# Attention scores computed twice in 32x64 tiles over four row strips and four PSUM banks, with norm rows on GpSimd

## The reference

```python
h = (tok_table[x] + pos_table + seg_table[seg]) * 16          # seg: cummax(x == 102)
h = h + attn(layernorm(h))
h = h + ffn(layernorm(h))
# attn: Q, K, V = x@wq, x@wk, x@wv in 16 heads of 16; a query sees the 64 keys up to itself
#   p = softmax(Q K^T / 4 masked to the window); local = p V
#   8 latent heads of 16 over 64 latents (means of 8 tokens of x@wgk, x@wgv), masked to the past
#   rem = softmax(GQ GK^T / 4) GV @ r_out_w
#   out = (sigmoid(Q.gate_l) * local + sigmoid(Q.gate_r) * rem) @ w_out
# ffn: each of 8 experts takes, in turn, the 2048 free tokens with the highest score norm(x)@centroid,
#   then routed + gelu(layernorm(routed)@w1 + b1)@w2 + b2, put back in the order of the tokens
```

## Time and profile before

| | |
|---|---|
| median of 3 runs | 5002.72 us (4962.28 to 5036.0) |
| span of the profiled execution | 4945.8 us |
| PE busy | 4629.6 us (94%), 27948 matmul records |
| PEld busy | 3051.0 us (62%) |
| DVE busy | 2406.4 us (49%) |
| ACT busy | 1623.1 us (33%) |
| POOL busy | 739.8 us (15%) |

### The profile page before, as it was taken

The page is one execution under the profiler, slowest core; times in us unless marked ns, Lnnn a source line. Parts: engine busy times, 40 slices in busy tenths (PEclk is TensorE's granted clock), DMA queues, the critical chain, the costliest instruction groups (busy, mean ns, idle before and its releaser), DMA issues. The chain is left out here.

```text
span 4945.8 us, 80440 instructions
## 1 busy us (share of the span) xinstructions
PE 4629.6 (94%) x27948; PEld 3051.0 (62%) x27948; DVE 2406.4 (49%) x7255; ACT 1623.1 (33%) x3333; POOL 739.8 (15%) x817
## 2 busy tenths in 40 slices
PE   5999999999999999999999999999996699999999
PEld 3666666666666666666666666666664366665666
DVE  4444444444444444534444444444445766666661
ACT  2333333333333333323333333333332233333333
POOL 1000000000000000100000000000000244444443
PEclk8777676776767676868676776767676799999999
DMA  1000000000000000000000000000000011111111
GB/s 36 14 10 10 10 11 10 10 9 10 11 10 9 10 11 10 15 9 11 10 11 10 10 10 10 10 10 10 10 11 27 20 51 52 47 50 51 48 42 41
DMA packets 52864, 94.25 MB, mean 19 GB/s; under 512 B 9116, under 2 KB 37736, under 8 KB 52488
## 3 DMA queue, kind: packets, MB, share of 16 engines
q0 software_dynamic: 18816, 51.41, 3.7%
q1 hardware_dynamic: 33672, 37.87, 2.3%
HBM read 55.68 MB, written 33.55 MB: 18 GB/s over the span
## 5 line engine op out<-in xcount | busy, mean ns | idle before, releaser
L1320 DVE TENSOR_REDUCE mx<-S_ps 128x4 f32<-128x512 f32 (+1 forms) x640 | 442.7, 692 | 1343.1 <-PE S_ps L914 1102.9
L914 PE MATMUL S_ps<-Kt,Qt 32*64 32x128 f32 (+1 forms) x6144 | 1090.7, 374 | 0.0
L687 ACT ACTIVATE probT<-T_ps 128x512 f32<-128x512 f32 x640 | 382.2, 597 | 1919.9 <-PE T_ps L963 1916.6
L914 PEld LDWEIGHTS S_ps<-Kt,Qt 32*64 32x64 f32 (+1 forms) x6144 | 634.0, 186 | 532.9 <-issue 463.9
L963 PE MATMUL T_ps<-cst,prob 128*128 128x128 f32 x2560 | 564.6, 360 | 0.0
L963 PEld LDWEIGHTS T_ps<-cst,prob 128*128 128x128 f32 x2560 | 381.9, 181 | 230.2 <-issue 230.2
L847 PE MATMUL S_ps<-hT,w 128*128 128x512 f32 x1024 | 474.7, 610 | 17.1 <-ACT hT L654 12.1
L860 PE MATMUL O_ps<-w,hid 128*128 128x256 f32 x2048 | 460.3, 379 | 0.0
L1321 DVE TENSOR_TENSOR prob<-S_ps,mx 128x512 f32<-128x512 f32 x640 | 442.6, 692 | 21.8
L936 PEld LDWEIGHTS O_ps<-Ve,probT 128*64 128x64 f32 x4096 | 359.8, 172 | 124.9 <-issue 124.9
L691 ACT ACTIVATE prob<-prob 128x512 f32<-128x512 f32 x640 | 401.0, 627 | 102.6 <-DVE prob L1321 102.2
(11 more groups left out here) (205 smaller groups left out, 5913.3 us busy)
## 6 DMA issues: line engine op xcount, KB each, us to landing
h_rows<-h SPq DMA_DIRECT2D x128, 128.0 KB, 1.7
w<-in_w SPq DMA_DIRECT2D x16, 1024.0 KB, 6.1
rows<-in_tok_table,idx_now POOLq DMA_INDIRECT x136, 3.6
out_rows<-orow,idx_cur POOLq DMA_INDIRECT x128, 2.4
b<-in_b SPq DMA_DIRECT2D x8, 128.0 KB, 5.1
hrow<-h_rows,idx_next POOLq DMA_INDIRECT x64, 2.8
hrow<-h_rows,idx_cur POOLq DMA_INDIRECT x64, 2.7
P<-in_pos_table SPq DMA_DIRECT2D x1, 512.0 KB
```

What stands on the lines that cost most here:

```text
L687: nc.scalar.activation(probT[u % 2][:, :], T_ps[u % 2][:, :], ACT.Copy).then_inc(s_pT, 1)
L914: mm = nc.tensor.matmul(cols[lo:hi, n:n + 2, a, :], Qt[par][r:r + 32, c, t * P + lo:t * P + hi], Kt[par][r:r + 32, c, block, :, :], start= ...
L1320: chain(dve, nc.vector.tensor_reduce(top, sc, AX.X, ALU.max), base)
```

## The change

The scores are computed twice, and the transposes of the probabilities go away. A sequence now has five units instead of 20: unit 0 is the latent heads of all four tiles, units 1 to 4 are all 16 heads of one tile each. A unit fills four PSUM banks (`banks`, formerly `S_ps` and `T_ps`), bank `g` from the 32 rows of strip `g` of the array.

First, `top_scores` computes the scores with queries on the partitions; DVE takes only their maxima (`dve_tops`, two instructions over 1024 columns each). PE transposes the maxima (task MX, eight output rows), ACT negates them into `low` or `lowl`, and SP copies them by DMA into a spare row of the queries. The matching row of the keys holds ones, so that a product of keys and queries has the maximum already taken off. Then `key_scores` computes the scores again, with keys on the partitions, into the same four banks, and ACT takes the exponential of them straight into `probT` (`act_exp`, two instructions over 1024 columns each). L1321, L963, L687 and the separate `scores` are gone. Masks are laid by bf16 matmuls of 32 rows and 64 output columns, 16 for each pass.

For each sequence, PE's program for the scores was 16 x (1 + 6) + 4 x 2 = 120 matmuls and 80 transposes. In the changed kernel `top_scores` is 16 masks and 64 matmuls of 64 columns for the latents, and 16 masks and 32 matmuls of 128 columns for each tile; `key_scores` is 16 masks and 8 matmuls of 512 columns for the latents, and 16 masks, 16 matmuls of 128 columns and 32 of 64 columns for each tile. That makes 160 masks, 392 fp32 matmuls and no transpose. All have the tile shape 32 x 64.

The other edits: `plan` has ten entries, two for each unit (one between `top_scores` and `key_scores`, one behind). The values of a whole tile are one task (VAL: 32 matmuls for heads and 8 for latents). POOL applies the norms itself (`pool_norm`, `pool_y`) and embeds two sequences ahead (`AHEAD`, `HB`, four buffers `hres`). Q, G and PK are written by ACT twice, once for each parity of the head. The loop's body is four sequences.

```diff
-RING = 4
-T_LAG = 2
-O_LAG = 3
+AHEAD = 3
+HB = 4
...
+        TAKER = {"ET": "A", "RT": "A", "RO": "D", "MT": "A", "WO": "D", "YT": "A", "SC": "D", "MX": "A",
+                 "Q": "A", "K": "A", "G": "A", "PK": "A", "PV": "D", "V": "A"}
...
+        plan = [
+            [("MT", 1), ("ET", 0), ("ET", 1), ("VAL", 2), ("ET", 2), ("ET", 3), ("YT", 0), ("WO", 1), ("MX", 0)],
+            [("RT", 2), ("Q", 0), ("SC", 0), ("RO", 2)],
+            [("MT", 2), ("VAL", 3), ("YT", 1), ("WO", 2), ("MX", 1)],
+            [("RT", 3), ("Q", 1), ("SC", 1), ("RO", 3)],
+            [("MT", 3), ("G", 0), ("PK", 0), ("YT", 2), ("WO", 3), ("MX", 2)],
+            [("K", 0), ("V", 0), ("SC", 2)],
+            [("VAL", 0), ("YT", 3), ("MX", 3)],
+            [("RT", 0), ("K", 1), ("PV", 0), ("SC", 3), ("RO", 0)],
+            [("MT", 0), ("VAL", 1), ("WO", 0), ("MX", 4)],
+            [("RT", 1), ("V", 1), ("V", 2), ("V", 3), ("RO", 1)],
+        ]
...
+                        if name == "MX" and m.here(task):
...
+                            sp.wait_ge(s_mA, m.out(task))
...
+                                    sp.dma_start(Qt[q % 2][HD * (1 - j)::32, j, :, (s - 1) * P:s * P],
+                                                 low[(s - 1) % 2][j::2, :, :]).then_inc(s_low[s], 16)
...
+        def pool_norm(pool, n, t, hb, m):
...
+            nc.gpsimd.tensor_tensor(out=rs0[:, t:t + 1], in0=ve0[:, t:t + 1], in1=mhalf[:, :],
+                                    op=ALU.pow).then_inc(s_rs0, 1)
...
+            nc.gpsimd.tensor_scalar(xn[:, t, :], hres[:, hb, t, :], mv0[:, t, 0:1], rs0[:, t:t + 1],
+                                    ALU.subtract, ALU.mult).then_inc(s_xn, 1)
...
+                            pool_y(pool, TS * (b - lag(task)), t)
...
+                    nc.scalar.activation(low[(t - 1) % 2][:, :, :], bank[0:2 * G, 0:KC * P].rearrange("p (c k) -> p c k", c=KC),
+                                         ACT.Copy, scale=-1.0).then_inc(s_mA, 1)
...
-                nc.scalar.activation(Qt[nx][:, t, :], bank[:, :], ACT.Copy, scale=HD ** -0.5).then_inc(s_mA, 1)
...
+                for j in range(2):
+                    ins_ = nc.scalar.activation(Qt[nx][:, j, t, :], bank[:, :], ACT.Copy, scale=c_query[:, j:j + 1])
+                ins_.then_inc(s_mA, 1)
...
+                    ins_ = nc.scalar.activation(Kt[nx][:, j, t, W:], bank[:, :], ACT.Identity,
+                                                scale=c_parity[:, j:j + 1], bias=c_unit[:, j:j + 1])
...
+        def act_exp(act, k, u, pair):
+
+            act.wait_ge(s_ST, 2 * k + pair + 1)
+            dst = latT if u == 0 else probT[(u - 1) % 2]
+            nc.scalar.activation(dst[:, 2 * pair:2 * pair + 2, :], banks[:, 2 * pair:2 * pair + 2, :],
+                                 ACT.Exp).then_inc(s_exp, 1)
...
-                        act.wait_ge(s_T, NUB * (b - back) + u + 1)
-                        nc.scalar.activation(probT[u % 2][:, :], T_ps[u % 2][:, :], ACT.Copy).then_inc(s_pT, 1)
...
-                        act.wait_ge(s_shift, 2 + NUB * b + s + 1)
-                        nc.scalar.activation(prob[:, s % RING, :], prob[:, s % RING, :], ACT.Exp).then_inc(s_exp, 1)
...
+                    first, rest = plan[2 * s + 1][0], plan[2 * s + 1][1:]
+                    run = m.old if s == 0 else m.new
+                    if run:
+                        act_exp(act, NU * b + s - 1, (s - 1) % NU, 0)
+                    act_misc(act, m, first, b, nx)
+                    if run:
+                        act_exp(act, NU * b + s - 1, (s - 1) % NU, 1)
+                    for task in rest:
+                        act_misc(act, m, task, b, nx)
...
+            elif name == "MX":
...
+                pe.wait_ge(s_max, 2 * (NU * b + t + 1))
+                if t == 0:
+                    tops = mxl[:, :].rearrange("p (g j t) -> p t (g j)", g=G, t=TS)
+                else:
+                    tops = mx[:, t % 2, :].rearrange("p (g j c) -> p c (g j)", g=G, c=KC)
+                for n in range(TS if t == 0 else KC):
+                    mm = nc.tensor.transpose(bank[0:2 * G, n * P:(n + 1) * P], tops[:, n, :], c_ident)
...
+            def top_scores(m, b, par, s):
...
+                if not (isinstance(b, int) and NU * b + s < 2):
+                    pe.wait_ge(s_exp, 2 * (NU * b + s - 1))
+                t = s - 1
+                for r in range(2):
+                    for g in range(G):
+                        for a in range(2):
...
+                                nc.tensor.matmul(banks[side[a], g, :].rearrange("p (h k) -> p h k", h=G),
+                                                 onehot[strip[g], r, :],
+                                                 by_query[strip[g], min(t, 1) if a == 0 else 1, r, :].unsqueeze(1)
+                                                 .to_broadcast([32, G, P]), start=r == 0, stop=False)
+                for n in range(2 * TS if s == 0 else G):
+                    j, c = divmod(n, TS if s == 0 else KC)
+                    for g in range(G):
+                        for a in range(2):
...
+                                at_ = t * P + a * W
+                                mm = nc.tensor.matmul(banks[side[a], g, n * P:(n + 1) * P],
+                                                      Qt[par][strip[g], j, c, at_:at_ + W],
+                                                      Kt[par][strip[g], j, c, at_:at_ + P],
+                                                      start=False, stop=n == G - 1)
+                        if g % 2 and n == (2 * TS if s == 0 else G) - 1:
+                            mm.then_inc(s_S, 1)
...
+            def key_scores(b, par, u, drained):
...
+                pe.wait_ge(s_max, drained)
+                pe.wait_ge(s_low[u], 32 * b + 32)
+                t = u - 1
...
+                if u == 0:
+                    for j in range(2):
+                        for g in range(G):
+                            mm = nc.tensor.matmul(banks[side[j], g, :], Gk[par][strip[g], j, :], Gq[par][strip[g], j, :],
+                                                  start=False, stop=True)
+                            if j and g % 2:
+                                mm.then_inc(s_ST, 1)
...
+                        nc.tensor.matmul(banks[side[0], g, n * P:(n + 1) * P], k[:, W + at_:P + at_], q[:, at_:at_ + P],
+                                         start=False, stop=n == G - 1)
+                        nc.tensor.matmul(banks[side[1], g, n * P:n * P + W], k[:, at_:W + at_], q[:, at_:at_ + W],
+                                         start=False, stop=False)
...
+                        mm = nc.tensor.matmul(banks[side[1], g, n * P + W:(n + 1) * P], k[:, P + at_:P + W + at_],
+                                              q[:, at_ + W:at_ + P], start=False, stop=n == G - 1)
+                        if n == G - 1 and g % 2:
+                            mm.then_inc(s_ST, 1)
...
+                        top_scores(m, b, par, s)
+                    half(2 * s)
+                    if m.old if s == 0 else m.new:
+                        drained = 2 * (NU * b + s + 1) if m.new else 2 * NU * SEQS
+                        if s == 0:
+                            key_scores(b - 1, 1 - par, NU - 1, drained)
+                        else:
+                            key_scores(b, par, s - 1, drained)
+                    half(2 * s + 1)
...
+        def dve_tops(dve, k, s):
+
+            for pair in range(2):
+                dve.wait_ge(s_S, 2 * k + pair + 1)
+                width = H if s == 0 else 2 * G
+                tops = mxl[:, pair * H:(pair + 1) * H] if s == 0 else mx[:, s % 2, pair * 2 * G:(pair + 1) * 2 * G]
+                nc.vector.tensor_reduce(tops.rearrange("p (g h) -> p g h", g=2),
+                                        banks[:, 2 * pair:2 * pair + 2, :].rearrange("p g (h k) -> p g h k", h=width // 2),
+                                        AX.X, ALU.max).then_inc(s_max, 1)
```

More of the change, by code:

```diff
@@ new lines, in _, with sequence @@
+            for t in range(TS):
+                pool_gather_rows(pool, 2, t)
+            for t in range(TS):
+                pool_norm(pool, 1, t, 1, Misc("head"))
+            def sequence(b, q):
+                m = Misc(b, q % 2)
+                ahead = not isinstance(b, int) or b + 2 < SEQS
+                for n, half in enumerate(plan):
+                    if ahead and n in EMBED_AT:
+                        pool_gather_rows(pool, b + 3, EMBED_AT[n])
+                    if ahead and n in NORM_AT:
+                        pool_norm(pool, b + 2, NORM_AT[n], (q + 2) % HB, m)
+                    for task in half:
@@ L711, in pe_misc @@
             name, t = task
-            if not m.here(task):
+            if name == "VAL" or not m.here(task):
                 return
@@ L926, in values @@
[L926 to L944 removed]
+            strip = [slice(32 * g, 32 * (g + 1)) for g in range(G)]
```

592 lines of the change are left out of this document (292 added, 300 removed).

## The result

| | before | after |
|---|---|---|
| median | 5009.3 us (4962.28 to 5036.0, 4 runs) | 3423.22 us (3416.55 to 3430.15, 4 runs) |
| span of the profiled execution | 4945.8 us | 3414.8 us |

A forecast was written before the change was run, and what follows sets the result against it. PE bounds the attention loop, 83.5 us a sequence at full clock. Kept work 37.7, scores 16, transposes 1.8 and waits 9.6 make 65 us, 78.3 at clock 0.78; 32 x 78.3 + 1234.4 + 57 gives 3800 us, range 3560 to 4350.

The forecast's parts named there:

- the clock: PE in the attention loop: mean clock 0.78, the trace's best sequences, so a sequence takes 78.3 us.
- the prediction's own formula: Attention sequence time 1/(w/65 + (1-w)/106), with w the time share at full clock and mean clock 0.5 + 0.5w.
- the share of projections grows: Reason given for attention's 0.78 clock: projections ran at 1.00 and fill more of a sequence as scores shrink.
- the 57 us: Whole kernel: median 5002.7 us over profiled span 4945.8 us, added to the new span of 3740 us.
- full clock throughout: Rival on PE's attention clock: full clock all the time, 3370 us; given no chance of its own.
- Under 3560, by a clock over 0.89: Outcome for the whole kernel: under 3560 us because PE's clock exceeds 0.89; chance 0.08.
- The scores: PE's score blocks: 12.8 us over eight tiles, raised to 13.8 by issue, plus 2.2 for shape changes: 16 us a sequence.
- within 1.5 to 2 us: Sign in PE's timeline: a tile's score block takes this long at full clock, matmul starts some 25 ns apart.
- The waits: PE waiting in attention for ACT's read-outs of Q, K, V and the bank for G and PK: 9.6 us a sequence.
- Work and waits at full clock: PE in an attention sequence: 55.5 us of work plus 9.6 us of waits, 65 us at full clock.
- POOL's norm rows and the small DMA releasing nobody: Sign in the attention profile: POOL's norms, 12 us more a sequence, and the maxima's DMA stay hidden.
- each late row would show on PE as a wait on `xn` or `y`: Attention norms moved to POOL: without several us of cover per row, PE would wait on these buffers.

The follow-up runs named there:

- strips in turn: Changed kernel with each block's score matmuls issued one row strip after another, masks and products the same: 5418.27 us, 1.10 of before.

## Why the prediction failed, and where it held

**The step that failed is the clock.** It says "so I take the better value, 0.78: w = 0.56 and 78.3 us". Measured: 0.957, so w = 0.91. Put into the prediction's own formula this gives 1 / (0.91/65 + 0.09/106) = 67.4 us, and 68.0 us were measured. The reason given, that the share of projections grows, is a small part: a tenth more work of that kind gave a clock of 0.74, and the time lost to the clock stayed as it was. What it left out is that the new scores, though each of their matmuls is narrow, would not hold the clock down when all four strips work at once: the same products keep the clock at 0.96 with four strips at once and at 0.64 with the strips in turn. How much of before's low clock was due to its scores and how much to its transposes stays open. The clock makes (78.3 - 68.0) x 32 = 330 us of the 377 us between forecast and measurement; most of the rest is the 57 us below. The rival "full clock throughout" (3370 us) was the nearest and had no chance of its own; "Under 3560, by a clock over 0.89" got 0.08.

**The scores** were sized at 16 us and take 17.3 us; a tile's block "within 1.5 to 2 us" takes 1.55 and 1.86 us. The pace of 25 ns of the earlier trace rows held in the latent `top_scores` (80 matmuls in 1.94 us, 24 ns each). It is 32 ns in a tile's `top_scores` (48 in 1.55 us) and 29 ns in its `key_scores`; the latent `key_scores`, with products over 512 columns, takes 1.77 us for 24. The Trainium skill ("TensorE: Matmul & The Clock Gate", "Wait — 56ns, not 53.3ns?") has 62 ns a matmul with hardware decode off; by that, an estimate, the 64 matmuls of a block would take 4 us. The trace has 1.86 us, so that pace doesn't bind in this run.

**The waits** were named rightly, with the read-outs of Q, K, G and V, but each is shorter than counted (1.0 against 1.6 us in RO), and K's stands in SC (L825) and not in RO. PE's in the sequence at 277.10:

```profile
PE M_ps L809 <- ACT Qt L673: 2.0, 2, 1.0
PE M_ps L825 <- ACT Kt L678: 1.7, 2, 1.1
PE M_ps L821 <- ACT Gq L683: 1.0, 1, 1.0
PE M_ps L806 <- DVE h L1208: 0.9, 2, 0.6
PE M_ps L844 <- ACT gt L695: 0.8, 1, 0.8
```

With the small ones some 7 us, for which 9.6 us were counted. Work and waits at full clock were forecast at 65 us, and the sequence takes 63.6 us. So that step held, in its mechanism and, within 2.5 us a term, in its sizes.

**Hidden by other work.** "POOL's norm rows and the small DMA releasing nobody" held: in the sequence at 277.10 no wait names `xn`, `y` or `low`. The rows read:

```profile
L1180 DVE TENSOR_REDUCE mx<-banks 128x8 f32<-128x1024 f32 x256 | 301.5, 1219 | 136.6 <-PE banks L1018 136.6
L701 ACT ACTIVATE probT<-banks 128x1024 f32<-128x1024 f32 x256 | 262.6, 1026 | 222.8 <-PE banks L1062 222.8
L528 POOL TENSOR_SCALAR xn<-hres,mv,rs 128x256 f32<-128x256 f32 x128 | 156.9, 1226 | 36.5 <-POOL rs L522 30.8 <-PE M_ps L844 2.0 <-PE M_ps L825 1.4
```

1.22 and 1.03 us against 1.4 and 1.1 us counted; POOL's row was put at 0.99 us and takes 1.23 us. The prediction also said that without that cover "each late row would show on PE as a wait on `xn` or `y`". With the rows on DVE none does: PE waits for the read-outs that stand behind them in DVE's order, and that costs 4.5%.

**The 57 us** between profiled span and median were carried over as if they were part of every launch. The changed kernel's profiled execution took 3416.55 us by the launch's time for a span of 3414.8, so the launch adds under 2 us, and the 57 us were the spread of the clock in before.

## What to carry over

Where PE sets the time, work out a change's length at full clock and its clock separately, and ask of the clock two things: how much of the array each stretch of matmuls fills at once, and how long PE's single waits become. Four strips of 32 rows in two column tiles, interleaved matmul by matmul, gave work and clock together; the same matmuls in turn lost both. In these kernels each idle moment over 1.6 us more went with 2.5 to 4.6 us more lost to the clock (an estimate from the table: the loss beyond that of the kernel it was made from, over the moments beyond its moments), so it is worth splitting such a wait, or moving the work that releases it (here out of DVE's order). The back edge's, with 14 to 17 us at half clock behind it, cost more.

## What was not expected of the hardware

- PE at 0.50 without an idle moment through a whole block of `key_scores`, 9.14 us, with one strip at a time (strips in turn). With all four strips at once 99 of 112 such blocks ran at 1.00 throughout.
- The back edge of PE's loop, with some 5550 matmul records in the body, stalls PE for 3.4 to 3.8 us, and 14 to 17 us at half clock follow it; neither is there with the loop written out. The Trainium skill ("TensorE: Matmul & The Clock Gate", Part 1) has idle time as what takes the clock back, and these rows agree. With strips in turn the clock fell in the middle of PE's work.
- Before, the same sequence of instructions ran at 0.68 or 0.78 from one iteration to the next, and at 0.73 or 0.84 with PE's loop written out, in repeating patterns. So its median is known to a per cent at best, while the changed kernel's four runs lie within 0.4%.
